# SiLU of the gate on ScalarE, in place of a tanh there and a multiply-add on VectorE

## The reference

```
x = LN(x + neighbourhood_attention(x))          # layer 0: 16 heads, 7 keys each, softmax
x = LN(x + gated_cross(x, ctx))                 # tanh over (token, key) pairs, softmax, two gates
x = LN(x + moe0(x))                             # 8 experts, top 2, SwiGLU   <- the change is here
x = LN(x + topk_attention(x))                   # layer 1: the 32 largest scores of each row
x = LN(x + cross_attention(x, ctx))             # softmax over 77 keys
x = LN(x + moe1(x))                             # 8 experts + 1 shared, exact GELU

moe0:  w = softmax(x @ gate_w.T); the 2 largest, divided by their sum -> ce[token, expert]
       g, u = split(x @ gate_up[e].T)           # 512 columns each
       out += ce[:, e] * ((silu(g) * u) @ down[e].T)
```

## Time and profile before

| what | value |
|---|---|
| median of three runs | 907.57 us (905.53 to 909.88) |
| span of the profiled execution | 905.5 us |
| TensorE matmul busy | 747.7 us, 4056 matmuls |
| VectorE busy | 609.4 us, 1568 instructions |
| ScalarE busy | 382.2 us, 619 instructions |
| `swiglu` with a next batch, e.g. batch 1 | about 331 to 433 us |
| `swiglu` of the last batch | about 723 to 802 us |

### The profile page before, as it was taken

How to read it: one execution, slowest core, us unless ns; L and a number is a source line. 1 busy time by engine, 2 the same in 40 slices (tenths; PEclk the granted TensorE clock), 3 DMA queues, 4 the chain that set the end, 5 groups by cost and what they waited for, 6 DMA issues and landing times.

```text
span 905.5 us, 12285 instructions
## 1 busy us (share of the span) xinstructions
PE 747.7 (83%) x4056; PEld 514.3 (57%) x4056; DVE 609.4 (67%) x1568; ACT 382.2 (42%) x619; POOL 101.4 (11%) x82
## 2 busy tenths in 40 slices
PE   3455739999997988989987988989988989973686
PEld 1210126776534875867344966876246978852576
DVE  3579957786494668885575678875755786749344
ACT  1035623216695442227785342238874332211142
POOL 2134312010002011020001120100011100000110
PEclk8759778999999899999999999999999999987578
DMA  6014100000000010000000010000000000000000
GB/s 234 0 47 169 51 5 24 0 1 1 2 1 2 1 42 1 1 1 1 1 3 0 2 41 1 1 1 1 1 3 1 1 13 1 1 1 0 1 1 12
DMA packets 6560, 15.14 MB, mean 17 GB/s; under 512 B 2776, under 2 KB 2912, under 8 KB 6240
## 3 DMA queue, kind: packets, MB, share of 16 engines
q1 hardware_dynamic: 6496, 14.32, 4.7%
HBM read 13.27 MB, written 1.05 MB: 16 GB/s over the span
## 4 chain that ended last, share of the span: by engine, by line
issue 65%; PE 13%; DVE 11%; POOL 7%; ACT 2%; DMA 1%; SPq 1%; POOLq 0%; DVEq 0%; ACTq 0%
DVE a_big L1362 4%; PE bank L633 3%; PE bank L494 1%; POOL b_rstd L1387 1%; PE bank L496 1%; PE bank L495 1%; PE bank L592 1%; POOL a_big L1397 1%; DVE top L1248 1%; POOL b_y L1413 1%; DVE b_big L1252 1%; ACT a_big L950 1%; POOL a_sum L1400 1%; POOL a_rstd L1383 1%; POOL gate_e L1407 1%
## 5 line engine op out<-in xcount | busy, mean ns | idle before, releaser
L868 ACT ACTIVATE b_big<-bank 128x512 f32<-128x512 f32 x128 | 75.7, 597 | 207.9 <-PE bank L496 207.7
L592 PE MATMUL bank<-a_big,score_pad 128*32 128x512 f32 x616 | 144.5, 650 | 22.2 <-ACT a_big L950 20.4
L837 ACT ACTIVATE a_big<-a_sum,txt_cols 128x512 f32<-128x512 f32 x231 | 145.5, 713 | 14.2 <-PE bank L592 14.1
L1210 DVE SCALAR_TENSOR_TENSOR b_big<-b_big,bank 128x512 f32<-128x512 f32 x128 | 87.2, 681 | 63.2 <-ACT b_big L868 59.0
L633 PEld LDWEIGHTS bank<-down_sb,b_big 128*128 128x128 f32 x1024 | 118.7, 192 | 6.1 <-issue 3.5
L494 PE MATMUL bank<-x_hi,gup_hi 128*128 128x512 f32 x256 | 112.4, 439 | 10.7 <-DVE b_big L1210 7.3
L633 PE MATMUL bank<-down_sb,b_big 128*128 128x128 f32 x1024 | 120.1, 276 | 0.0
L496 PE MATMUL bank<-x_lo,gup_hi 128*128 128x512 f32 x256 | 104.2, 407 | 0.0
L495 PE MATMUL bank<-x_hi,gup_lo 128*128 128x512 f32 x256 | 104.1, 407 | 0.0
L592 PEld LDWEIGHTS bank<-a_big,score_pad 128*32 128x32 f32 x616 | 26.7, 111 | 118.2 <-ACT a_big L837 54.7
L1216 DVE TENSOR_TENSOR b_big<-bank,b_big 128x512 f32<-128x512 f32 x128 | 88.5, 691 | 4.4
(11 more groups left out here) (214 smaller groups left out, 975.9 us busy)
## 6 DMA issues: line engine op xcount, KB each, us to landing
b_big<-gup SPq DMA_DIRECT2D x8, 512.0 KB, 7.6
down_sb<-down SPq DMA_DIRECT2D x1, 2048.0 KB, 8.3
rw_sb<-rw SPq DMA_DIRECT2D x1, 1152.0 KB, 10.6
a_T<-x_T SPq DMA_DIRECT2D x4, 256.0 KB, 2.6
a_tok<-x_tok SPq DMA_DIRECT2D x4, 256.0 KB, 3.1
b_big<-rw SPq DMA_DIRECT2D x2, 512.0 KB, 3.6
y<-b_tok SPq DMA_DIRECT2D x4, 256.0 KB, 2.0
const_sb<-const SPq DMA_DIRECT2D x1, 872.0 KB
```

Of the source, the lines that this page charges most:

```text
L592: last = mm(P[2][32 * j:32 * j + 32, :], score_pad[:, 31 - i:63 - i], ring[k % RING], start=(i == 0), stop=(KCOL * (i + 1) + j >= KEYS))
L837: act(ring[k % RING], a_sum[:, 0:S], ACT.Tanh, bias=txt_cols[:, c:c + 1])\
L868: act(th[n % 3], P[3 + 2 * (c % 2)][:, :], ACT.Tanh, scale=0.5).then_inc(th_ready, 1)
L1210: stt(th[n % 3], th[n % 3], 1.0, P[3 + 2 * (c % 2)][:, :], ALU.add, ALU.mult)\
```

## The change

ScalarE writes silu(g) itself into the same SBUF tile. The scalar_tensor_tensor of line 1210 goes, and with it the semaphore `t1_done` and VectorE's wait for its own result; VectorE still waits for `th_ready` before the multiply by u. TensorE's g bank is now released by ScalarE's `th_ready`. The factor 0.5 goes from the routing weights, whose last instruction becomes a plain multiply of the same size. Nothing is moved in any engine's order.

```diff
--- before.py
+++ after.py
@@ -369,7 +369,6 @@
         g_psum = sem("g_psum")
         u_psum = sem("u_psum")
         th_ready = sem("th_ready")
-        t1_done = sem("t1_done")
         hid_ready = sem("hid_ready")
         down_psum = sem("down_psum")
         part_ready = sem("part_ready")
@@ -637,7 +636,7 @@
                 for e in range(E):
                     for c in range(C0):
                         n = e * C0 + c
-                        for half, bank, freed, ready in ((0, P[3 + 2 * (c % 2)], t1_done, g_psum),
+                        for half, bank, freed, ready in ((0, P[3 + 2 * (c % 2)], th_ready, g_psum),
                                                          (1, P[4 + 2 * (c % 2)], hid_ready, u_psum)):
                             if n >= 2:
                                 eng.wait_ge(freed, E * C0 * b + n - 1)
@@ -865,7 +864,7 @@
                         eng.wait_ge(g_psum, E * C0 * b + n + 1)
                         if n >= 3:
                             eng.wait_ge(hid_ready, E * C0 * b + n - 2)
-                        act(th[n % 3], P[3 + 2 * (c % 2)][:, :], ACT.Tanh, scale=0.5).then_inc(th_ready, 1)
+                        act(th[n % 3], P[3 + 2 * (c % 2)][:, :], ACT.Silu).then_inc(th_ready, 1)
                         if n == 0:
                             route_exp(b, 0)
                         if ahead:
@@ -1185,8 +1184,7 @@
                 eng.reciprocal(r_den[:, :], r_den[:, :]).then_inc(share_step, 1)
                 eng.wait_ge(share_step, n + 3)
 
-                stt(r0_we, r0_we, 0.5, r_den[:, :].unsqueeze(2).broadcast_to(r_wide), ALU.mult, ALU.mult)\
-                    .then_inc(r_weights, 1)
+                tt(r0_we, r0_we, r_den[:, :].unsqueeze(2).broadcast_to(r_wide), ALU.mult).then_inc(r_weights, 1)
 
 
             def swiglu(b, ahead):
@@ -1207,9 +1205,6 @@
                     for c in range(C0):
                         n = e * C0 + c
                         eng.wait_ge(th_ready, E * C0 * b + n + 1)
-                        stt(th[n % 3], th[n % 3], 1.0, P[3 + 2 * (c % 2)][:, :], ALU.add, ALU.mult)\
-                            .then_inc(t1_done, 1)
-                        eng.wait_ge(t1_done, E * C0 * b + n + 1)
                         eng.wait_ge(u_psum, E * C0 * b + n + 1)
                         if c == 0 and e >= 2:
                             eng.wait_ge(down_psum, E * b + e - 1)
```

## The result

The kernel after takes 893.87 us (median of four runs, 891.16 to 894.58), the kernel before on the same chip 906.55. The ratio is 0.9856, 95% interval [0.9834, 0.9877], that is 13.1 us faster with an interval of 11.2 to 15.0 at 906.55. Forecast were 12.1 us and 895.5.

A forecast was written before the change was run, and what follows sets the result against it. TensorE, busy 83% of the span, was taken as pacing the kernel. VectorE terms of 15.7 us plus 1.8 for the clock, less 5.4 for table loads, gave 12.1 us net: 895.5 us, range 886 to 917.

The forecast's parts named there:

- VectorE's late start and the product gap: Batch start and score products: less VectorE backlog saves 2.0 and 2.1 us in batches 1 and 2, 1.7 in batch 0.
- The clock: TensorE's half clock around the product gap costs 1.8 us in each of two batches; half of 3.6 taken as gain.
- Step 15 and the chain of the sum: Step 15's wait for line 1210 goes, 0.5 us; less backlog ahead of the attention sum's last product, 0.4 us.
- The transposes after step 23: Transposes waiting for the LayerNorm, which comes over 1 us earlier: 0.8 us a batch, bounds 0.27 and 1.19.
- The last batch: Step 2: the g bank is free at once and u starts where g did: 0.7 us gained.
- the likeliest case: Silu's set holds Tanh but not Exp: 18 more table loads, costing 5.4 us in all; chance 0.50.
- Step 13: Exp's loads after step 10 delay step 11's Silu; TensorE waits 1.2 us for that bank.
- A: Rival: Silu is in Exp's set, so no table load is added: 890 us; chance 0.16.
- B: Rival: Silu's set lacks Tanh, so steps 24 to 31 switch too, 5.3 us per batch: 909.6 us; chance 0.13.
- C: Rival: as B but dearer, 8.5 us per batch, through score matmuls and Tanh linked both ways: 919 us; chance 0.13.
- D: Rival: VectorE's gain is given back at later waits, 5 us left against 5.4 of loads: 907; chance 0.06.
- E: Rival: each table switch costs 1.36 us more than the 1.30 seen, 7.0 per batch: 911 us; chance 0.02.

The follow-up runs named there:

- Experiment 3: Kernel after plus a 0.68 us VectorE instruction, read by nobody, behind each multiply by u: 906.42 us, ratio to the kernel before 0.9977.
- experiment 4: Kernel after with the g bank released by VectorE's hid_ready in place of ScalarE's th_ready: 899.91 us, ratio to the kernel before 0.9912.
- experiment 2: Kernel before with Silu in place of Tanh and line 1210 kept, so only the table switches are added: 915.51 us, ratio 1.0094.
- experiment 5: Kernel after with ScalarE's Exp of the scores after step 9 in place of step 10: 887.78 us, ratio to the kernel before 0.9779.
- experiment 1: Kernel after with unscaled Tanh where Silu stands, so no table loads are added: 888.17 us, ratio to the kernel before 0.9790.
- experiment 8: Kernel after with a one-column Exp ahead of each Tanh group of swiglu, nine more loads per batch: 907.34 us, ratio to the kernel before 1.0002.
- experiment 7: Experiment 6 with the attention's spread, products and sum one step earlier, output unmoved: 887.54 us, ratio to the kernel before 0.9778.
- experiment 9: Experiment 7 with the sum's three adds kept at step 18 in place of 17: 881.57 us, ratio to the kernel before 0.9712.
- experiment 6: Experiment 5 plus a one-column Exp ahead of ScalarE's part of the cross attention: 887.75 us, ratio to the kernel before 0.9787.

## Why the prediction was right, by its steps

- VectorE's late start and the product gap: 4.1 us forecast for batches 1 and 2, 1.7 for batch 0. g0 to score fell by 3.8, 4.4 and 1.6, 9.7 in all for 9.9. Experiment 3 gives the cause: with VectorE's time taken up again the gap is back.
- The clock: 1.8 was taken as half of 3.6. With the gap gone the second score matmuls came 1.26 and 1.24 us sooner behind the first in batches 0 and 1, and not in batch 2, where the clock had not fallen. Some 0.3 more a batch lies behind the second score (37.22 and 37.28 before, 36.99 in batch 2). So a fall cost about 1.5 us and not 1.8, and both went: 3.1 for 1.8.
- Step 15 and the chain of the sum: 0.9 a batch. Without loads the stretch fell by 1.33, 1.39 and 1.10, of which some 0.3 in the first two is the clock's: 1.1.
- The transposes after step 23: 0.8 in three batches. It was 0.87 in batches 1 and 2 (turn to b_tok) and in batch 0 nothing, where the transposes had not waited before either (0.60 us long at 206.88, 0.92 in batch 1). There I took the pattern of batch 1 for all. And it isn't VectorE's backlog: experiments 3 and 4 keep this gain, while experiment 2, with line 1210 on the chain, has 34.92 in batches 0 and 2 (34.04 in batch 1). Batch 0's out to turn is 1.6 shorter for another reason, which no term of the prediction had: in the kernel before its matmuls from 198.10 to 199.81 stand 0.43 us apart, at a granted clock of 0.50 (1.2 GHz), and after the change they don't.
- The last batch: 0.7 forecast, 1.43 seen. The u matmul starts where the g matmul did (6.03 us from g0, 6.02 before), as foreseen, and the g matmuls ahead of it are the 0.7. The prediction overlooked the stage's end, where 0.55 of the other 0.7 lies. From the seventh `down_mm` to the last is 12.54 us before and 11.99 after, and before, line 1210 holds up a g matmul there:

```profile
792.28 0.50 PE L494 MATMUL bank<-x_hi,gup_hi 128*128 128x512 f32 x1 [0.26 <-DVE b_big L1210]
```

Experiment 2, with line 1210 kept, has the same wait of 0.26 at 800.22. Experiments 3 and 4 don't have it. Over the whole stretch, profiles with the clock's fall at step 2 compare as 83.48 before and 82.05 after, those without it as 82.00 (experiment 2) and 80.50 (experiment 5).

- ScalarE's instruction: 597 ns, as Tanh had.
- The tables: the likeliest case, load for load, 18 more. Step 0: 0, as forecast. Step 13: 1.2 forecast for the bank and 1.65 measured. The g matmul of step 13 comes 1.19 us later than without loads (experiment 1), the `down_mm` 1.55 and the step's end 1.66: the term of the bank was right, and what stands behind it was left out. Line 909: 0.6 forecast, 0.62 measured. Together 6.8 for 5.4.
- Both halves were a little too small, 19 for 17.5 and 6.8 for 5.4, and the two misses cancel: 13.1 for 12.1. The hit on the sum is better than its terms, and so partly luck: the clock falls alone were worth some 4.7 us (3.1 and 1.6) in the profile before (two product gaps and batch 0's output), where the prediction had 1.8.

One sentence of the prediction was wrong in its reason: 905.5 is the span, and the profiled execution's time lies around 2 us above it (891.16 for a span of 889.3 after the change). The 2.1 us added to reach the forecast were this, and not the spread between runs.

The rivals. A (no loads) fell by the trace; it would have given 888 (experiment 1), 890 by its working. B and C fell by the trace as well; B's price was right (experiment 8), and the change would then have been worth nothing; its sum of 5.3 a batch stands against 5.56 measured. D (908 by its own terms, written as 907) fell: g0 to b_tok of batch 1, by the table, went from 106.66 to 100.99 us. E fell: a switch takes 1.31 us from activation to activation (136.21 to 137.52 in batch 0) and no idle time follows it. So the drain in the Trainium skill (ScalarE: Activation LUTs, "What ACT_TABLE_LOAD costs") is not seen in this kernel, while its 1283 ns for the load is exact. The same page's table of sets ("Table sets: the hidden batching unit") has tanh beside exp and beside sigmoid; here it is in silu's set too, which that table doesn't list.

## What to carry to other kernels

Price the removal of an instruction from an engine by who waits for that engine: 91 us of VectorE work were worth 19, and a spare instruction as long, off the chain and read by nobody, took 11 of them back. The rest came from where the instruction had stood: on the chain, holding a bank (experiment 2 against 3, 10.6 us). Before swapping an activation function, walk through ScalarE's program and count where its set is left and re-entered; a switch's 1.3 us count only where TensorE wants what is behind it, and moving one Exp by one step, in front of a stretch in which ScalarE is idle, made the worst of them free. When a wait is removed by moving work, look what now stands behind the moved work on its own engine (experiments 7 and 9 differ by one number).

## What the runs showed of the hardware

- ACT_TABLE_LOAD isn't held back by the wait of the activation that it is for: it starts 0.02 us after the activation before it (352.19 in experiment 5) and the wait comes behind it (1.98 us there). All the loads of the kernel after but the first of the program start 0.02 us after the activation before them. So a load costs nothing where the engine would have waited as long anyway.
- The set that an activation leaves loaded serves all later ones that it holds: with a one-column Exp ahead, the Tanh groups run out of Exp's set and the cross attention's Exp needs no load (experiments 6 and 8). So a tiny activation places a load where one wants it.
- After an idle time of 1.76 us on TensorE its matmuls ran at 1.2 GHz (granted 0.50 from 365.0 to 368.2) in batch 1 of experiment 4 and not in batches 0 and 2, which have the same wait. The granted clock falls after some such gaps and not after others, for some 1.5 us of loss each time: product gap and batch 0's output before the change, step 2 of the last batch in most profiles (82.05 for 80.50 us). Closing a gap is worth that on top, sometimes.
- The same work can take 34.65 or 36.25 us in one kernel by where the stretch at 1.2 GHz lies in it (the Gelu stage). Before a difference of 1 to 2 us between two profiles is put down to an edit, compare the granted clock of the stretch.
